# Where a pair's 36 edge lookups stand among the matmuls of a fused graph and expert kernel

## What is computed

```
xn  = layernorm(x)
ft  = xn @ W                         # 4 heads of 64
e   = leaky_relu(e_src[src] + e_dst[dst]),  e_src = sum(ft*att_src), e_dst = sum(ft*att_dst)
a   = softmax of e over the edges of one dst, times dist
x   = x + segment_sum(ft[src] * a, dst)
xn  = layernorm(x);  w = softmax(mean(xn) @ Wr + br)     # here per node, batch of one
for 8 experts: h = relu(bn(xn @ W1)); h = relu(bn(h @ W2)); y = h @ Wo + bo
x   = x + sum over experts of w * y
```

## Time and profile before

| | us |
|---|---|
| median of 3 runs | 1673.95 |
| the profiled execution | 1672.18 |
| its span | 1670.6 |

### The profile page before, as it was taken

How to read it: one execution, slowest core, us unless ns; L and a number is a source line. 1 busy time by engine, 2 the same in 40 slices (tenths; PEclk the granted TensorE clock), 3 DMA queues, 4 the chain that set the end, 5 groups by cost and what they waited for, 6 DMA issues and landing times.

```text
span 1670.6 us, 23915 instructions
## 1 busy us (share of the span) xinstructions
PE 1488.4 (89%) x8358; PEld 1292.6 (77%) x8358; DVE 1213.7 (73%) x2207; ACT 777.6 (47%) x1353; POOL 1028.3 (62%) x926
## 2 busy tenths in 40 slices
PE   2664035999999999999999999999999999999998
PEld 2442034888888888888888888888888888888887
DVE  3333266887888888888888888788778877887751
ACT  1232013455545554555555545555555555455543
POOL 1000777777777777777777777777777777777000
PEclk9887556999999999999999999999999999999999
DMA  3332934444443444344444444444444344433000
GB/s 116 104 103 79 303 111 112 128 115 129 111 128 103 129 112 128 103 129 112 122 112 121 118 115 119 114 123 111 123 115 125 106 125 114 125 105 109 20 0 13
DMA packets 106040, 187.48 MB, mean 112 GB/s; under 512 B 38454, under 2 KB 70475, under 8 KB 105890
## 3 DMA queue, kind: packets, MB, share of 16 engines
q0 software_dynamic: 43664, 121.77, 26.5%
q1 hardware_dynamic: 55264, 57.76, 11.5%
q10 hardware_dynamic: 6992, 6.42, 1.3%
HBM read 172.72 MB, written 14.42 MB: 112 GB/s over the span
## 4 chain that ended last, share of the span: by engine, by line
PE 66%; DVE 11%; issue 7%; DMA 6%; POOL 4%; ACT 4%; SPq 0%; DVEq 0%; ACTq 0%; POOLq 0%
PE bankH L701 33%; PE bankY L730 16%; PE bankE L660 5%; PE bankE L661 5%; POOL gath L565 4%; DMA gath<-in_x 4%; ACT msg_hi L866 3%; DVE onehot L1237 2%; PE bankE L596 2%; PE bankB L646 1%; DVE x L1348 1%; DVE stats L1297 1%; DVE x L1295 1%; DVE x L1291 1%; PE bankA L678 1%
## 5 line engine op out<-in xcount | busy, mean ns | idle before, releaser
L565 POOL DMA_INDIRECT gath<-table,src_win x900 | 1020.9, 1134 | 502.4 <-issue 229.4
L894 ACT ACTIVATE h<-bankH,bn_shift,bn_scale 128x250 f32<-128x250 f32 x800 | 401.5, 552 | 424.6 <-PE bankH L701 424.3
L701 PE MATMUL bankH<-h,w 128*128 128x250 f32 x1600 | 446.6, 398 | 0.0
L730 PE MATMUL bankY<-wo,h 128*125 128x256 f32 x1600 | 378.1, 379 | 1.1 <-DVE x L1348 1.1
L701 PE MATMUL bankH<-xT,w 128*128 128x250 f32 x1600 | 375.2, 377 | 0.1
L1279 DVE TENSOR_TENSOR msg_lo<-gath,msg_hi 128x2340 fp32r<-128x2340 f32 x100 | 259.5, 2595 | 114.3 <-ACT msg_hi L866 114.3
L730 PEld LDWEIGHTS bankY<-wo,h 128*125 128x125 f32 x1600 | 296.0, 187 | 42.5 <-issue 1.4
L866 ACT ACTIVATE msg_hi<-gath 128x2340 fp32r<-128x2340 f32 x100 | 215.1, 2151 | 233.0 <-PE bankE L661 229.6
L701 PEld LDWEIGHTS bankH<-xT,w 128*128 128x128 f32 x1600 | 294.2, 190 | 30.4 <-ACT h L894 0.2
L701 PEld LDWEIGHTS bankH<-h,w 128*128 128x128 f32 x1600 | 278.4, 198 | 18.0 <-issue 0.2
L1348 DVE SCALAR_TENSOR_TENSOR x<-bankY,gate,x 125x256 f32<-125x256 f32 x400 | 173.9, 475 | 136.4 <-PE bankY L730 136.4
(11 more groups left out here) (164 smaller groups left out, 870.1 us busy)
## 6 DMA issues: line engine op xcount, KB each, us to landing
onehot_t<-dst_low SPq DMA_DIRECT2D x50, 576.0 KB, 5.2
gath<-table,src_win POOLq DMA_INDIRECT x900, 2.8
x_res<-in_x SPq DMA_DIRECT2D x27, 250.0 KB
table<-gath SPq DMA_DIRECT2D x25, 253.9 KB
out<-x SPq DMA_DIRECT2D x25, 250.0 KB
gath<-in_x SPq DMA_DIRECT2D x23, 250.0 KB
w<-in_L_ffn_W ACTq DMA_DIRECT2D x2, 2048.0 KB, 21.6
wo<-in_L_ffn_Wo ACTq DMA_DIRECT2D x1, 2048.0 KB, 37.3
```

The costliest lines, as they stand in the source:

```text
L565: pool.indirect_dma_start(gath[:, g.slot(u), t, :], None, table, bass.IndirectOffsetOnAxis(src_win[:, g.win, u, t:t + 1], 0)).then_inc(row ...
L701: mm = pe.matmul(target[:, hc * 2 * NT:(hc + 1) * 2 * NT], weights[:, e * KC + c, hc * P:(hc + 1) * P], operand(c), start=(c == 0), stop=( ...
L730: mm = pe.matmul(bankY[0:NT, u * D:(u + 1) * D], h2[:, e % 2, c, u, :], wo[:, e * KC + c, :], start=(c == 0), stop=(c == KC - 1))
L894: ins = act.activation(target[:, e % 2, hc, :, :].rearrange("p u n -> p (u n)"), source[:, hc * 2 * NT:(hc + 1) * 2 * NT], ACT.Relu, bias= ...
```

## The change

The lookups are taken out of the second layers. In stages with experts all 36 are issued in one run in step 3, between `turn_bounds` and layer 2; layer 2 gets `nothing` in every step. The stages without experts are as before. In `BEHIND` the rows of steps 3 and 4 are exchanged: step 3 now allows two gather rows behind layer 2 and step 4 one.

```diff
--- before.py
+++ after.py
@@ -33,7 +33,7 @@
 SLOTS = 4
 WINS = 4
 FROM = 5
-BEHIND = ((1, 1, 1, 0), (1, 1, 2, 0), (1, 1, 1, 2), (1, 1, 1, 2), (1, 2, 1, 2), (1, 1, 1, 2), (1, 1, 2, 0), (1, 1, 2, 0))
+BEHIND = ((1, 1, 1, 0), (1, 1, 2, 0), (1, 1, 1, 2), (1, 2, 1, 2), (1, 1, 1, 2), (1, 1, 1, 2), (1, 1, 2, 0), (1, 1, 2, 0))
 SEG = 2 * H
 TS = TE + 1
 CHUNKS = 4
@@ -738,11 +738,6 @@
 
             def body(f, g, a):
                 small = to_edges(a) if a is not None else iter(())
-
-                def between():
-                    for _ in range(2):
-                        next(small, None)
-
                 for s in range(EX):
                     if f is not None:
                         layer1(f, s, nothing)
@@ -752,17 +747,17 @@
                             out_bias(f)
                     if a is not None and s == 3:
                         turn_bounds(f, a)
+                    if s == (3 if f is not None else 1):
+                        for _ in small:
+                            pass
                     if f is not None and (s >= 1 or not f.begins(1)):
-                        layer2(*before(f, s, 1), between if 1 <= s <= 6 else nothing)
+                        layer2(*before(f, s, 1), nothing)
                     if f is not None and s == 1:
                         turn_gate(f)
                     if g is not None and s == (7 if f is not None else 6):
                         turn_x1(g)
                     if f is not None and (s >= 2 or not f.begins(1)):
                         layer3(*before(f, s, 2), nothing)
-                    if s == (6 if f is not None else 1):
-                        for _ in small:
-                            pass
                     if g is not None and 2 <= s < 2 + CHUNKS:
                         aggregate(g, s - 2)
                     if a is not None and s == 6:
```

## The result

| | before | after |
|---|---|---|
| median, us | 1672.5 (4 runs) | 1683.32 (4 runs, 1681.81 to 1685.58) |
| the profiled execution | 1672.18 | 1683.11 |
| its span | 1670.6 | 1681.5 |

The ratio is 1.0071, with a 95% interval of 1.0058 to 1.0084. The change makes the kernel slower by 10.8 us. The forecast was 1658.8 with a range of 1650 to 1670: the sign is wrong, and the time is outside the range.

A forecast was written before the change was run, and what follows sets the result against it. TensorE was taken as the pace from L628 to the third aggregation, VectorE from there to the next L628. Terms -1.02 + 0.68 - 0.35 = -0.69 us a pair, times 22 = 15.2, gave 1658.8 against the median 1673.95; range 1650 to 1670.

The forecast's parts named there:

- The block: All 36 lookups in one run on TensorE: 35 spacings of 0.03 us plus 0.14, together 1.19 us.
- the way back: Last lookup and the long matmul behind it, whose loads could not be fetched ahead: 0.14 us, paid once, not 18 times.
- step 3: TensorE's step that receives all 36 lookups: loses 0.51 us, gets 1.19, so +0.68 us a pair.
- The rival: Lookups in a row cost 0.062 us at either clock, a fixed issue time per matmul; pair +0.43, 1683 us; chance 0.08.
- The price by columns: Rival: every load in a row is paid by its columns, 0.12 us each; pair +2.5 us, 1713 us; chance 0.02.
- Steps 1 and 2: In TensorE's own part, six lookups fewer in each: 2 x 0.51 = 1.02 us a pair, all gained.
- Step 4: Loses 0.51 us of lookups; only 0.35 a pair gained, the remaining 0.16 becoming a wait for VectorE's low halves.
- the drain: The last pair, run without lookups beside it; its 7.44 us against 7.79 gave the 0.35 gain.
- Steps 5 and 6: In VectorE's part: 1.02 us less TensorE time, gain 0; wait at L628 grows to about 1.1 us a pair.
- The exchange in `BEHIND`: One gather row moves from step 4's allowance to step 3's, covered by GpSimd's slack; priced at 0.
- SP and GpSimd: SP's reloads of the transposed one-hots and GpSimd's gathers and pacing were expected to delay nothing; priced at 0.
- The first pair: First pair with experts, said to run behind its gathers: given no gain, 0 to 1 us in the forecast's range.

The follow-up runs named there:

- g3_step5: The changed kernel with the 36 lookups moved ahead of step 5's aggregation and the old BEHIND order; 1648.67 us, ratio 0.9858 to the kernel before.
- e1_contig: The changed kernel with each lookup's 128 one-hot columns side by side, not 18 apart (output wrong); lookups 0.025 us apart, 0.88 us first to last; whole time not given.

## Why the prediction was wrong

**The step that failed is "The block".** It took 0.03 us a lookup, as "the nearest row in clock and place", after halving the 0.062 of the cold blocks to the higher clock. The cold block was the right row, and halving it was the error: its spacing is that of reading 128 columns 36 bytes apart, and is 0.062 at either clock. The 0.030 between the two lookups of a group was no price of a lookup either. It is there in the block too, between the first and the second only, at any distance of the columns; the load of the second is paid behind it, as 0.059 of the way back that I had put at 0.14. With 2.14 in place of 1.05 the term is 1.09 larger, and step 3 is +1.77 where +1.76 was measured. (The six lookups gave back 0.46 there and not 0.51, and the block cost 2.22 and not 2.28: both differences are the same 0.05, which `g3_step5`, without lookups in step 3, spends ahead of the second aggregation, 1.59 us from layer 3's start to it where the kernel after has 1.54.)

**The rival had the number, not the reason.** Its 1683 is the measured time, and its 0.062 the measured spacing. But it said that each matmul costs a time to issue, and `e1_contig` issues the same 36 at 0.025. My argument against it (18 matmuls and 18 loads passed by the sequencer in 0.3 us) was sound, and I let it carry away the number 0.062 as well, which a second row, the cold block, supported on its own. A chance of 0.08 was too low for a value that stood in the trace. That its 1683 is met so closely is luck in part: it has +0.43 a pair where +0.36 was measured, and nothing for the 2.7 us that come on top by the end of the first pair, 1.7 of them in the stretch with the halved clock.

**The price by columns was 1728, not 1713.** The rival with 0.12 us a load adds up to 54 us, and 1674 + 54 is 1728; the text has 1713. Nothing else hangs on it.

**A rule that I did not weigh.** The Trainium skill's rule on lines of 16 bytes (Advanced Engine Details and Errata, "SBUF Cachelines") concerns exactly this operand, `onehot_t[0:NT, u, t:WIN:TE]`. It gives no figure for a weight load, but it would have given the cold 0.062 a reason that has no clock in it. I set against the trace only the Trainium skill's price of a load by its columns, an estimate of 107 ns, which neither the columns side by side (25 ns) nor those far apart (61 ns) confirm, and with half the columns the load takes longer.

**The other steps held.**
- Steps 1 and 2: -1.02 forecast, -1.03 measured.
- Step 4: -0.35 forecast, -0.25 measured. `g3_step5` has -0.28, so taking the drain for it was off by 0.07 to 0.1.
- Steps 5 and 6: 0 forecast, -0.11 measured, with the wait at L628 at 1.1 a pair as forecast. This is the part that the block's place decides.
- The exchange in `BEHIND`: 0 forecast. The aggregations stand where they should with either order, and no run shows a value for it. What it is worth alone on a chip without the stall was not measured.
- SP and GpSimd: 0 forecast, and no wait of TensorE names them. GpSimd's busy time rises from 1028.3 to 1076.3, since its gathers, whose mean is 1188 ns after 1134, stand longer; nothing waits for that.
- The first pair: given nothing, it is 2.0 us longer, 1.7 of them in the stretch with a granted clock of 0.50, and begins 1.1 late.

**What the change was worth without its place.** Taking the lookups out of the second layers saves TensorE 18 x 0.172 = 3.1 us a pair and the block costs 2.2. That is a gain of 0.9, and `g3_step5` collects it, 1.03 a pair with the wait at L628 gone as well. The changed kernel puts the whole 2.2 into the part where TensorE sets the pace, and takes a third of the savings, those of steps 5 and 6, from the part where VectorE does.

## What to carry to other kernels

Work that is gathered from many places into one block should stand where another engine sets the pace; read for each stretch between two recurring starts who releases the next one, and price both the old places and the new one by that. When short matmuls follow each other, the load of the weights can be their price: look at the distance between its columns first; for bf16 here up to 6 bytes were nearly free. And a duration may be scaled with the clock only if a row shows the same operation at both levels.

## What was not expected of the hardware

- Loads of 128 bf16 columns, each with a matmul of 12 moving columns, start every 25 ns with the columns 2 to 4 bytes apart, 33.5 at 8, 46.7 at 12, 57 to 61 from 16 bytes on; at 36 bytes 48 moving columns take no longer.
- At granted clocks of 1.00 and 0.50 the pace is nearly the same: 25.1 and 26.8 ns side by side, 61.2 and 61.8 at 36 bytes.
- 64 columns take 121 ns, twice the time of 128 at the same distance.
- A long f32 matmul behind two short bf16 ones is followed 0.083 us later than usual, with the columns of the short ones at 2 or at 36 bytes.
- One wait of TensorE of 2.6 us was followed by a granted clock of 0.50 in the kernel after, and cost 1.7 us more; one of 1.6 us in the kernel before was not.
- Chips differ: the kernel before takes 1671 to 1673 us in two groups of runs and 1704 to 1708 in four others, and a block at the end of step 6 takes 1655 on one chip and 1825 on another. An order of instructions that is faster on one chip has to be timed on several; `g3_step5` was timed on one.

A kernel with right results and its one-hot columns side by side was not tried. VectorE makes `onehot_t` in place from the row that SP loads, so it would need a second buffer, 9 KB a partition, or a row that is loaded in that order.
